# Storing the split gate and up quarters of a weight step in the first pair of blocks and loading them for the second

## What is computed

```
x = x + ffn(layernorm(x))
gate[e] = x @ Wg[e] (+ x @ Ga[e] @ Gb[e] for e < 2)      # 512 x 512 weights
up[e]   = x @ Wu[e] (+ x @ Ua[e] @ Ub[e] for e < 2)
mid[e]  = silu(gate[e]) * up[e]
out[e]  = mid[e] @ Wd[e] (+ mid[e] @ Da[e] @ Db[e] for e < 2)
ffn     = sum over e of router_weight[e] * out[e]
```

## Time and profile before

| | |
|---|---|
| median of 3 runs | 1064.21 us (1063.29 to 1064.3) |
| the profiled execution | 1064.18 us |
| its span | 1062.4 us |
| TensorE (PE) busy | 1045.8 us, 98% |
| VectorE (DVE) busy | 712.2 us, 67% |
| ScalarE (ACT) busy | 447.8 us, 42% |
| GpSimd (POOL) busy | 55.4 us, 5% |
| moved by DMA | 94.73 MB, 89 GB/s over the span |
| granted TensorE clock | 0.998 of 2.4 GHz |

### The profile page before, as it was taken

One profiled execution on the slowest core, in us unless ns is written; L12 is line 12 of the kernel. 1 busy time (PEld: TensorE's weight loads), 2 busy tenths in 40 slices (PEclk: granted clock), 3 DMA queues, 4 the chain that ended last, 5 costly groups with the idle time before them and its releaser, 6 DMA issues.

```text
span 1062.4 us, 12255 instructions
## 1 busy us (share of the span) xinstructions
PE 1045.8 (98%) x4696; PEld 856.8 (81%) x4696; DVE 712.2 (67%) x1212; ACT 447.8 (42%) x647; POOL 55.4 (5%) x66
## 2 busy tenths in 40 slices
PE   7899999999999999999999999999999999999998
PEld 5777878887888888888888888788888888888887
DVE  6779587968485765848477684938556474837544
ACT  3663442555253344425334344524434442524430
POOL 2621111100000000000000000000000000000000
PEclk9999999999999999999999999999999999999999
DMA  9401104145142241514225446212021121112012
GB/s 319 130 10 40 80 1 179 40 139 159 38 138 54 90 118 60 159 50 133 57 94 184 136 143 214 63 40 74 26 80 41 60 60 58 42 40 73 27 40 80
DMA packets 88667, 94.73 MB, mean 89 GB/s; under 512 B 4384, under 2 KB 62880, under 8 KB 87712
## 3 DMA queue, kind: packets, MB, share of 16 engines
q1 hardware_dynamic: 87456, 90.73, 27.0%
q0 software_dynamic: 864, 3.15, 1.0%
q10 hardware_dynamic: 288, 0.07, 0.0%
HBM read 76.63 MB, written 17.30 MB: 88 GB/s over the span
## 4 chain that ended last, share of the span: by engine, by line
PE 89%; DVE 5%; ACT 2%; issue 2%; DMA 1%; POOL 1%; SPq 0%; DVEq 0%; POOLq 0%
PE gate_up L1592 16%; PE gate_up L1593 16%; PE gate_up L1594 16%; PE tiles L1479 10%; PE tiles L1480 10%; PE tiles L1481 10%; PE gate_up L1550 2%; PE gate_up L1551 2%; PE gate_up L1556 2%; DMA first_raw_all<-in_wu_dram 1%; PE tiles L1515 1%; DVE mids_lo L1241 1%; POOL w_lo L569 1%; PE gate_up L1487 1%; DVE xacc L1215 1%
## 5 line engine op out<-in xcount | busy, mean ns | idle before, releaser
L1592 PE MATMUL gate_up<-xT_hi,piece_hi 128*128 128x512 f32 x448 | 174.9, 390 | 1.1 <-DVE mids L1202 0.6
L1479 PE MATMUL tiles<-wd_hi,mids_hi 128*128 128x512 f32 x448 | 174.4, 389 | 0.4 <-DVE mids_lo L1241 0.4
L1594 PE MATMUL gate_up<-xT_lo,piece_hi 128*128 128x512 f32 x448 | 174.3, 389 | 0.0
L1593 PE MATMUL gate_up<-xT_hi,piece_lo 128*128 128x512 f32 x448 | 174.3, 389 | 0.0
L1480 PE MATMUL tiles<-wd_lo,mids_hi 128*128 128x512 f32 x448 | 174.3, 389 | 0.0
L1481 PE MATMUL tiles<-wd_hi,mids_lo 128*128 128x512 f32 x448 | 174.3, 389 | 0.0
L1215 DVE SCALAR_TENSOR_TENSOR xacc<-tiles,rw,xacc 128x512 f32<-128x512 f32 x112 | 78.0, 750 | 139.0 <-PE tiles L1481 139.0
L1163 DVE TENSOR_TENSOR piece_lo<-piece,piece_hi 128x1024 fp32r<-128x1024 f32 x112 | 118.2, 1097 | 28.6 <-ACT piece_hi L791 27.2
L1592 PE MATMUL gate_up<-tx_hi,piece_hi 128*128 128x512 f32 x336 | 130.8, 389 | 0.0
L1593 PE MATMUL gate_up<-tx_hi,piece_lo 128*128 128x512 f32 x336 | 130.7, 389 | 0.0
L1594 PE MATMUL gate_up<-tx_lo,piece_hi 128*128 128x512 f32 x336 | 130.7, 389 | 0.0
(11 more groups left out here) (172 smaller groups left out, 1419.6 us busy)
## 6 DMA issues: line engine op xcount, KB each, us to landing
piece<-in_wg_dram SPq DMA_DIRECT2D x40, 256.0 KB, 3.2
piece<-in_wu_dram SPq DMA_DIRECT2D x40, 256.0 KB, 3.3
wd_raw<-in_wd_dram SPq DMA_DIRECT2D x10, 1024.0 KB, 5.1
piece<-merged SPq DMA_DIRECT2D x32, 256.0 KB, 3.2
merged<-lora_w SPq DMA_DIRECT2D x6, 1024.0 KB, 4.3
x_back<-x_spill SPq DMA_DIRECT2D x9, 512.0 KB, 5.2
wd_raw<-merged SPq DMA_DIRECT2D x4, 1024.0 KB, 5.4
out_dram<-xacc SPq DMA_DIRECT2D x16, 256.0 KB, 4.1
```

The source lines that it names most:

```text
L1479: nc.tensor.matmul(dst, w_h, x_h, start=first, stop=False)
L1592: nc.tensor.matmul(dst, w_h, x_h, start=first and kt == 0, stop=False, skip_group_check=True)
L1593: nc.tensor.matmul(dst, w_l, x_h, start=False, stop=False, skip_group_check=True)
L1594: ins = nc.tensor.matmul(dst, w_h, x_l, start=False, stop=last and kt == 1, skip_group_check=True)
```

## The change

Two groups of three semaphores (`piece_stored`, `piece_back`) and one DRAM tensor (`piece_spill`, 28 pieces x 2 halves x 128 x 1792 float32) are added. For pieces 0 to 27 GpSimd's queue stores `piece_hi` and the seven used slots of `piece_lo` as soon as the piece is ready. For pieces 28 to 55 SyncE's queue loads these halves in place of the raw weights, and VectorE's and ScalarE's work on them is left out. A piece set is overwritten only when its store has landed.

```diff
+        piece_spill = nc.dram_tensor("piece_spill", [4 * SWAP, 2, P, 7 * 2 * P], fp32, kind="Internal").ap()
...
+        def piece_halves(j):
+            return plain(piece_hi[j % 3][:, :, :]), plain(piece_lo[j % 3][:, 1:8, :])
+
+        def spilled(j, part):
+            return piece_spill[j % (4 * SWAP), part, :, :].rearrange("p (g c) -> p g c", g=7)
...
+            def load_piece_back(j):
+                for part, halves in enumerate(piece_halves(j)):
+                    sp.dma_start(halves, spilled(j, part)).then_inc(piece_back[j % 3], 16)
+
             def load_next_piece(j):
 
                 if j < 4 * STEPS:
                     sp.wait_ge(p_mm[4], j - 2)
-                    load_piece(j)
+                    if j - 3 < 4 * SWAP:
+                        sp.wait_ge(piece_stored[j % 3], 32 * (j // 3))
+                    if j < 4 * SWAP:
+                        load_piece(j)
+                    else:
+                        load_piece_back(j)
...
             pool.wait_ge(x_stored, 64)
+            def store_piece(j):
+                pool.wait_ge(piece_ready[j % 3], j // 3 + 1)
+                for part, halves in enumerate(piece_halves(j)):
+                    pool.dma_start(spilled(j, part), halves).then_inc(piece_stored[j % 3], 16)
+
+            for j in range(4 * SWAP):
+                store_piece(j)
             load_again(0, 0, 1)
...
             def piece_high_part(j):
-                if j < 4 * STEPS:
+                if j < 4 * SWAP:
...
             def piece_sums(j):
 
-                if j >= 4 * STEPS:
+                if j >= 4 * SWAP:
                     return
...
             def piece_low_part(j):
-                if j >= 4 * STEPS:
+                if j >= 4 * SWAP:
                     return
...
-                pe.wait_ge(piece_ready[j % 3], j // 3 + 1)
+                if j < 4 * SWAP:
+                    pe.wait_ge(piece_ready[j % 3], j // 3 + 1)
+                else:
+                    pe.wait_ge(piece_back[j % 3], 32 * ((j - 4 * SWAP) // 3 + 1))
```

More of the change, by code:

```diff
@@ L284, in xattn_ffn_kernel @@
         piece_ready = [sem(f"piece_ready{i}") for i in range(3)]
+        piece_stored = [sem(f"piece_stored{i}") for i in range(3)]
+        piece_back = [sem(f"piece_back{i}") for i in range(3)]
         wd_loaded = sem("wd_loaded")
```

## The result

The changed kernel takes **1068.07 us** (median of 6 runs, 1067.15 to 1068.46) against 1064.07 (6 runs, 1063.29 to 1064.47) for the kernel before: ratio 1.0037, 95% interval [1.0027, 1.0048]. It is 4.0 us slower, by more than the 0.2% that the text ahead took as what a measurement can tell, and above the predicted range, which ends at 1067.6. The profiled execution took 1068.46 us, its span is 1066.5 and its mean granted clock 0.996. (One execution in this study, of the kernel with stores alone, took 1769 us at a mean granted clock of 0.557, which nothing here explains; it is left out of that kernel's median and ratio.)

A forecast was written before the change was run, and what follows sets the result against it. TensorE, busy 98% of the span, was taken as the bound. The profiled 1064.18 us, less 1.7 for three waits, plus 1.5 for the loop's start, gave 1064.0 us; the range was 1062.3 to 1067.6.

The forecast's parts named there:

- All 1.72 us should go: -1.7: Second pair: three TensorE waits of 0.69, 0.48 and 0.55 us, in steps 6 and 7, should all go.
- the first gap: 624.50 to 625.31, end of `down_half(6, 0)`: TensorE waits for VectorE's low half of mid; 0.69 us to go.
- the other two: At 671.46 and 676.05, `quad`s of pieces 31 and 32: waits for `copy_p5` and `make_mid`, 0.48 and 0.55 us to go.
- the loads by themselves: Second pair: larger loads of 1.835 MB per piece fit before the `quad` needing them, cost 0; piece 32 tightest.
- 9.4 was the bound: Second pair: a piece's load takes at most 9.4 us, against at least 25.8 us available in a regular step.
- busy time, bytes, the burst: Signs: VectorE 108 and ScalarE 48 us less busy, about 182 MB moved, DMA share about 1.0 from 212 to 234.
- the term of +1.5: Start of the loop: two stores fall where the DMA engines are full, delaying piece 3's load; cost 1.5 us.
- Slack 1.55: Step 0, `Wd` chain: VectorE's sum ends at 227.34, the product needing it starts at 228.89; cost 0 to 1.5 us.
- up to 3.1 us of work ahead of or beside `Wd`: Step 0: how much work of the first store may stand before or beside the load of `Wd`.
- I take a landing between, at 232.5, a cost of +1.5.: Step 0, piece 3's load: no slack, free if landed by 231, at most 4.9 us for landing at 235.8.
- the 0 for the stores after the start: First pair's regular steps and the swap: the stores and SyncE's new wait for them cost 0.
- (a): Rival: at the start both stores get ahead of piece 3, price 4.9, net +3.2, 1067.3 us; chance 0.24 with smaller risks.

The follow-up runs named there:

- the kernel with stores alone: The change with all 28 pieces stored, but the second pair loading and splitting raw weights as before: 1069.35 us, ratio 1.0055.
- the loads alone: The change with only piece 0 stored and all 28 second-pair loads bringing piece 0's halves (results wrong): 1062.35 us, ratio 0.9987.
- the change's two profiles: The changed kernel's own profile (1068.07 us, ratio 1.0037) and one from running the same instructions once more (1068.25 us, ratio 1.0042).
- store 1 alone: The kernel before plus only the two DMAs that store piece 1, never read again: 1069.75 us, ratio 1.0051.
- the run with only the first one held: The change with only the store of piece 1 held until Wd of step 0 has landed: 1064.14 us, ratio 0.9996.
- short rows: The kernel before plus only piece 1's store, the same bytes in rows of 512 B: 1074.16 us, ratio 1.0091.

## Why the prediction was wrong

**Right: the gain.** "All 1.72 us should go: -1.7". They went, and the loads alone measure it (-1.7 us in the medians, 853.6 against 855.4 in the loop). The split by place holds too: piece 28 for the first gap, piece 32 for the other two.

**Right: the loads by themselves.** "0", from the rows for transfer times and slack. No matmul waits for `piece_back`. The medians from issue to landing are 4.5 and 6.4 us, where 9.4 was the bound. What the prediction did not have is that the load of piece 28, beside the stores of step 6, delays the `Wd` behind it.

**Right: busy time, bytes, the burst.** 96.6 and 42.6 us less busy against 108 and 48, 182.8 MB against 182, and engines full from 212 to about 233 against 234.

**Wrong: the price at the start, the term of +1.5.** The place was right and the chain was not. The step that failed is the slack of `Wd`: "the fourth product of piece 1, at 228.89, needs that sum. Slack 1.55." The kernel before shows, in TensorE's timeline:

```profile
227.16 0.39 PE L1594 MATMUL gate_up<-tx_lo,piece_hi 128*128 128x512 f32 x1
227.40 0.50 PE L1592 MATMUL gate_up<-tx_hi,piece_hi 128*128 128x512 f32 x1
227.73 0.40 PE L1593 MATMUL gate_up<-tx_hi,piece_lo 128*128 128x512 f32 x1
```

In the earlier trace rows the matmul at 228.89 is the next product, the sixth, which belongs to piece 2. A product is six matmuls, 1.36 us, and this one has a first matmul that is 0.11 longer; so the fourth product of piece 1 starts 1.49 us earlier, at 227.40, and VectorE's sum (226.66 and 0.68) ends at 227.34. The slack was 0.06. Names of tiles do not tell products apart, and I took a row for the product instead of counting products from the start of the piece. With the right slack, my own bound of "up to 3.1 us of work ahead of or beside `Wd`" would have been near the price: 2.75 and 3.32 us in the change's two profiles. (The bound has no working; from the terms beside it, 5.4 us for a store less the 2 that pass before the burst, it would be 3.4.)

**Right in size by luck, and still not a term: piece 3.** "I take a landing between, at 232.5, a cost of +1.5." In the change VectorE waits for it until 233.00, which is 232.3 when the loop's later start (0.72) is taken off. The changed kernel, SyncE's queue and VectorE:

```profile
224.22 3.15 SPq L376 DMA_DIRECT2D piece<-in_wu_dram  x2
...
233.00 0.42 DVE L1176 TENSOR_TENSOR piece<-piece 128x256 f32<-128x256 f32 x1 [2.19 <-DMA piece<-in_wu_dram]
```

The prediction had the loads in time and the stores in their way. In fact SyncE's queue waits for the accumulators' store before it goes on, and this store lands 7.7 us after its issue (4.9 before), so the loads of piece 3 go out 2.9 us later (224.22 against 220.62, less 0.72). By then the second store is ahead of them, and they land after 7.5 us, against 4.5 before and 4.8 with store 1 alone. That the second store gets ahead is due to the first, as the run with only the first one held shows. And the two costs do not add up: TensorE has lost 2.75 us to `Wd` by then, and `quad` 3 starts at 239.66, again 2.75 later than before, counted from the loop's start. The price of the start is the larger of the two.

**Wrong: the 0 for the stores after the start.** It rested on "In the regular steps a step's 7.3 MB take 20 us of its 61.7." A mean over a step says nothing of a wait inside it. I had gone through the waits of SyncE's queue for `piece_stored`, and not through those that it already had: the merged weights' store of step 6, on which it stands. With the store of piece 24 that wait is 3.1 to 3.5 us longer than in the kernel before, and VectorE's line had less room than that: TensorE lost 1.67 us by it in the first profile and 1.0 in the second. The 0.63 of the small gap come on top in the first.

**Not foreseen: the clock.** After the pauses of 3.45 to 7.65 us in step 0 TensorE ran at half the clock, which cost 1.6 us three times and 2.4 once.

The rival that came nearest is (a): slower, by the burst at the start, put at 1067.3 with a chance of 0.24. Its mechanism, both stores ahead of piece 3, did happen, and it was not what cost the time. The two wrong terms make the error: 2.75 us at the start and 2.3 in step 6 in the first profile, 4.9 (with the clock) and 1.0 in the second, are 5.05 and 5.9 where the prediction had 1.5, so 3.6 and 4.4 more, against the 4.1 us between 1064.0 and 1068.07.

## What to carry to other kernels

Where one engine is at 98%, list its gaps before adding anything: here 2 pieces of 28 carried the gain, and each of the other stores could gain nothing and could meet a chain without slack. Count the slack of a chain to the start of the right instruction, found by the loop's structure and not by equal names, and go through every wait on every queue that shares the DMA engines, not only the ones that the change adds. A store with no one waiting for it belongs behind the load that someone waits for.

## What the runs showed of the hardware

**The clock after a pause.** In step 0 pauses of 3.45, 3.55, 4.02 and 7.65 us (start to start) were each followed by 3 to 5 us of matmuls 0.43 us apart in place of 0.227, with a granted clock down to 0.50, the 1.2 GHz level. In the longest pause the clock was at 0.50 already while TensorE stood; after the one of 4.02 us the first matmuls still came at the old pace. The pause of 2.98 us in the change's first profile had no such stretch behind it. TensorE's timeline with the single store:

```profile
232.75 0.47 PE L1631 MATMUL gate_up<-tx_lo,piece_hi 128*128 128x512 f32 x1
233.03 0.63 PE L1629 MATMUL gate_up<-tx_hi,piece_hi 128*128 128x512 f32 x1
233.45 0.63 PE L1630 MATMUL gate_up<-tx_hi,piece_lo 128*128 128x512 f32 x1
```

Eight matmuls at that distance cost 1.6 us here, so the price of these waits of 3.2 to 3.8 us went up by about a half. The change had this in one of its two profiles.

**Issues on SyncE took longer beside GpSimd's stores.** SyncE's issue of `Wd` took 0.44 us before and 1.26 in the change, 0.66 with store 1 alone and 1.65 with it in short rows. The issue of piece 3's two loads took 3.15 us in the change, behind the second store. Full engines alone do not do it: that issue took 1.14 before, at a DMA share of 1.04, and 1.14 with store 1 alone, when that store was through. Why it is so no run here tells.

**Short rows cost twice.** The same 1.84 MB took 18.3% of 16 engines over 25 us in rows of 7 KB and 26.0% in rows of 512 B, that is 4.6 and 6.5 us of all of them, and the other queue's unchanged 3.15 MB went from 43.5% to 48.8%.
